# Causal attention on one NeuronCore: DRAM bounce laid out by component and head, first keys transposed into VectorE's PSUM bank

## What is computed

```python
q = einsum('bsm,hmd->bshd', resid, W_Q) + b_Q      # 32 heads of 32
k = einsum('bsm,hmd->bshd', resid, W_K) + b_K
v = einsum('bsm,hmd->bshd', resid, W_V) + b_V      # 256 values, 8 per head
q = _apply_rotary(q, sin, cos, 32)
k = _apply_rotary(k, sin, cos, 32)
k = concatenate([k, virtual_k], axis=1)            # 16 more keys
v = concatenate([v, virtual_v], axis=1)
scores = einsum('bqhd,bkhd->bhqk', q, k) / sqrt(32)
mask = arange(s + 16)[None, :] <= arange(s)[:, None] + 16
pattern = softmax(where(mask, scores, -inf), axis=-1)
z = einsum('bhqk,bkhr->bqhr', pattern, v_grouped)
out = einsum('bqhd,hdm->bqm', z, W_O)
```

## Time and profile before

| | us |
|---|---|
| median of 3 runs | 1694.87 |
| lowest and highest | 1694.71, 1704.96 |
| the profiled execution | 1699.04 |
| its span, from the first to the last instruction | 1697.2 |

### The profile page before, as it was taken

The page is one execution under the profiler, slowest core; times in us unless marked ns, Lnnn a source line. Parts: engine busy times, 40 slices in busy tenths (PEclk is TensorE's granted clock), DMA queues, the critical chain, the costliest instruction groups (busy, mean ns, idle before and its releaser), DMA issues. The chain is left out here.

```text
span 1697.2 us, 36694 instructions
## 1 busy us (share of the span) xinstructions
PE 1473.9 (87%) x12580; PEld 938.1 (55%) x12580; DVE 1234.0 (73%) x3703; ACT 1119.9 (66%) x2657; POOL 440.1 (26%) x442
## 2 busy tenths in 40 slices
PE   4688998989989885588888888769999999999996
PEld 2255555556555553366666666646555555555564
DVE  4367777777777765688888788663877878878755
ACT  1267676776767761567777677627888787887742
POOL 0333333333333313454544444330000000000001
PEclk9599999999999997899999999877999999999998
DMA  1677777788777745111001110007999999999920
GB/s 41 163 185 194 188 186 197 185 194 190 186 186 189 194 108 187 22 30 31 19 20 31 25 27 19 12 13 219 324 315 315 309 314 300 313 314 302 292 73 25
DMA packets 154904, 272.97 MB, mean 161 GB/s; under 512 B 27920, under 2 KB 31200, under 8 KB 154592
## 3 DMA queue, kind: packets, MB, share of 16 engines
q1 hardware_dynamic: 154720, 270.63, 56.3%
HBM read 148.03 MB, written 112.98 MB: 154 GB/s over the span
## 5 line engine op out<-in xcount | busy, mean ns | idle before, releaser
L519 ACT ACTIVATE a_Pm<-a_Pm,a_nm 128x272 f32<-128x272 f32 (+3 forms) x512 | 266.7, 570 | 167.3 <-DVE a_nm L441 166.7
L441 DVE CUSTOM_DVE_ANT_0 a_Pm<-ps,a_mask 128x272 f32<-128x272 f32 (+3 forms) x512 | 237.7, 503 | 92.3 <-PE ps L358 90.8
L1768 ACT COPY r_BD<-ps 128x320 f32<-128x320 f32 x512 | 200.4, 428 | 92.1 <-PE ps L1621 46.7
L1895 DVE CUSTOM_DVE_ANT_0 r_Sx<-ps,r_Sx 128x512 f32<-128x512 f32 x256 | 176.8, 691 | 108.8 <-PE ps L1634 107.2
L1621 PE MATMUL ps<-r_R,r_qv 32*128 32x320 f32 x1024 | 234.2, 498 | 3.2 <-ACT r_BD L1768 2.3
L358 PE MATMUL ps<-a_Kst,a_Qst 128*128 128x272 f32 (+4 forms) x640 | 200.6, 409 | 15.4 <-DMA a_Kst<-bounce 15.1
L1634 PE MATMUL ps<-r_K,r_qu 32*128 32x256 f32 x1024 | 199.7, 436 | 3.4 <-DVE r_nb L1895 3.4
L358 PEld LDWEIGHTS ps<-a_Kst,a_Qst 128*128 128x128 f32 x640 | 113.4, 193 | 146.3 <-issue 62.6
L1775 ACT ACTIVATE r_Sx<-r_Sx,r_nb 128x512 f32<-128x512 f32 x256 | 187.6, 733 | 7.9 <-DVE r_nb L1895 7.9
L1904 DVE COPY r_PT<-ps 128x512 f32<-128x512 f32 x256 | 175.9, 687 | 4.6 <-PE ps L1644 4.0
L373 PE MATMUL ps<-m_ident,a_Pm 128*128 128x128 f32 x1280 | 170.5, 278 | 1.6 <-ACT a_Pm L519 0.7
(11 more groups left out here) (204 smaller groups left out, 2745.9 us busy)
## 6 DMA issues: line engine op xcount, KB each, us to landing
spill<-r_BD SPq DMA_DIRECT2D x256, 288.0 KB, 5.0
r_Sx<-spill SPq DMA_DIRECT2D x128, 512.0 KB, 5.7
a_Kst<-bounce SPq DMA_DIRECT2D x128, 264.0 KB, 4.9
a_Qst<-bounce SPq DMA_DIRECT2D x128, 256.0 KB, 4.6
bounce<-a_kh SPq DMA_DIRECT2D x32, 264.0 KB, 3.5
bounce<-a_kl SPq DMA_DIRECT2D x32, 264.0 KB, 4.1
bounce<-a_qh SPq DMA_DIRECT2D x32, 256.0 KB, 5.7
bounce<-a_ql SPq DMA_DIRECT2D x32, 256.0 KB, 6.0
```

The lines of the kernel that those rows point to most:

```text
L441: nc.vector.tensor_tensor_reduce(out=Pm[:, u % 2, qt, 0:w], in0=S[:, S_of[qt]:S_of[qt] + w], in1=mask[:, N + AV - w:N + AV], scale=-SCALE, ...
L519: nc.scalar.activation(row, row, ACT.Exp, scale=-1.0, bias=nm[:, u % 2, qt:qt + 1]).then_inc(exp_done, 1)
L1768: nc.scalar.copy(BD[:, m % BUFS, j, HW * half:HW * half + HW], ps[:, BDB[k % 3], 0:HW]).then_inc(bd_ev, 1)
L1895: nc.vector.tensor_tensor_reduce(out=row, in0=ps[:, AC + n % 2, :], in1=row, scale=-SCALE, scalar=-BIG, op0=ALU.add, op1=ALU.min, accum_ou ...
```

## The change

Four things are rewritten, and no instruction is added or removed.

- `bounce` becomes (half, component, head, position) instead of (half, partition, position), and the tensors for queries have rows of 512 instead of 528.
- The stores to it now run over a destination view `h c n`: for each head, 32 components, one row each. The source is the same 128 partitions.
- `Qst` and `Kst` swap head and batch, so that the four heads of a batch lie side by side in a partition; a load reads one run of 4 x 512 or 4 x 528 numbers per component and writes one run per partition. The scores matmuls index accordingly.
- `first_transposes` writes to bank `TB + 1` and waits for VectorE's count `evd` instead of ScalarE's `eva`; the wait for `p0_ev`, which guards what follows in that bank, moves from part 0 of a unit's transposes to part 1.

```diff
-    Qst = [s.sb(f"Qst{i}", [P, GH, NB, N], F32R) for i in range(2)]
-    Kst = [s.sb(f"Kst{i}", [P, GH, NB, KN], F32R) for i in range(2)]
+    Qst = [s.sb(f"Qst{i}", [P, NB, GH, N], F32R) for i in range(2)]
+    Kst = [s.sb(f"Kst{i}", [P, NB, GH, KN], F32R) for i in range(2)]
...
-    bounce = [[nc.dram_tensor(f"bounce{k}{m}", (2, P, KN), F32, kind="Internal").ap() for m in range(4)] for k in range(2)]
+    bounce = [[nc.dram_tensor(f"bounce{k}{m}", (2, AD, GH, (N, KN)[m % 2]), F32, kind="Internal").ap() for m in range(4)] for k in range(2)]
...
             def stack(st, m):
                 i, k = m // 2, 4 * st + m
-                width_ = (N, KN)[m % 2]
                 dst, halves = ((Qst, (qh, ql)), (Kst, (kh, kl)))[m % 2]
                 for j, (src, made) in enumerate(zip(halves, (hi_done, lo_done))):
                     sp.wait_ge(made, k + 1)
-                    sp.dma_start(bounce[st % 2][m][j, :, 0:width_], src[:, i].bitcast(F32)).then_inc(bounced, 16)
+                    sp.dma_start(bounce[st % 2][m][j].rearrange("c h n -> h c n"), src[:, i].bitcast(F32)).then_inc(bounced, 16)
                 sp.wait_ge(bounced, 32 * (k + 1))
                 if st >= 2:
                     sp.wait_ge(s_ready, 2 * (U * (st - 2) + GH * (i + 1)))
                 for block, j in enumerate(((0, 1, 0, 1), (0, 0, 1, 1))[m % 2]):
-                    sp.dma_start(dst[st % 2][32 * block:32 * block + 32, :, i].bitcast(F32),
-                                 bounce[st % 2][m][j, :, 0:width_].rearrange("(h c) n -> c h n", h=GH)).then_inc(stk[st % 2][i], 16)
+                    sp.dma_start(dst[st % 2][32 * block:32 * block + 32, i].rearrange("c h n -> c (h n)").bitcast(F32),
+                                 bounce[st % 2][m][j].rearrange("c h n -> c (h n)")).then_inc(stk[st % 2][i], 16)
...
-                        ins = nc.tensor.matmul(S[:, lo:lo + w], q[:, h, i, P * qt:P * qt + P], k[:, h, i, at:at + w],
+                        ins = nc.tensor.matmul(S[:, lo:lo + w], q[:, i, h, P * qt:P * qt + P], k[:, i, h, at:at + w],
...
                     pe.wait_ge(exp_done, 4 * u + 4)
                     if u >= 1:
                         pe.wait_ge(evd, u)
+                    if u >= GH and u % GH == 1:
+                        pe.wait_ge(p0_ev, u // GH)
                 elif u >= 1:
                     pe.wait_ge(eva, 2 * u - (1 if k == 2 else 0))
-                if k == 0 and u >= GH and u % GH == 1:
-                    pe.wait_ge(p0_ev, u // GH)
...
                 pe.wait_ge(p0_done, GH * (bb + 1))
-                pe.wait_ge(eva, 2 * min(GH * (bb + 1) + 1, UNITS))
+                pe.wait_ge(evd, min(GH * (bb + 1) + 1, UNITS))
                 for qt in range(NT):
-                    ins = nc.tensor.transpose(ps[:, TB, P * qt:P * qt + P], P0[:, bb % 2, qt, :], c["ident"][:])
+                    ins = nc.tensor.transpose(ps[:, TB + 1, P * qt:P * qt + P], P0[:, bb % 2, qt, :], c["ident"][:])
...
-                nc.vector.tensor_copy(P0T[:], ps[:, TB, :]).then_inc(p0_ev, 1)
+                nc.vector.tensor_copy(P0T[:], ps[:, TB + 1, :]).then_inc(p0_ev, 1)
```

## The result

| | median us | runs | ratio to before, 95% interval |
|---|---|---|---|
| before | 1698.08 | 4 | |
| changed | 1948.69 (1945.62 to 1954.28) | 4 | 1.1474 [1.1423, 1.1524] |

The changed kernel is 251 us slower. (A fourth run of the kernel before moved its median from 1694.87 to 1698.08.) The forecast was slower with a chance of 0.92, at 2174 us, in a range of 1905 to 2255. So direction and range held, and the time forecast was 225 us too long; rival 1, with 1925 us, came closer than the forecast. The profiled execution of the changed kernel took 1954.28 us, its span is 1952.5.

A forecast was written before the change was run, and what follows sets the result against it. It took SP's serial chain of transfers in the attention stage as the bound. 483 - 3 - 1 = +479 us on the profiled 1699.04 gave 2178, less 4.2 for the median: 2174 us, range 1905 to 2255.

The forecast's parts named there:

- rival 1: Bounce stores: four engines don't collide, each at full 24.6 GB/s; pair 5.4 us, +3.65 per link, 1925 us; chance 0.25.
- What bounds the kernel: Attention stage: SP's serial chain of stack loads and bounce stores sets the pace, 63 links of 8.81 us; compute keeps up closely.
- The count of engines: Bounce stores: a destination of 4 outermost puts each store on four of the 16 DMA engines.
- The rate of four engines: Bounce stores: colliding engines take 9.3 us for a pair instead of 1.75; +7.55 us per link, +483 us over 64 pairs.
- The stack loads: Loads into Qst and Kst: longer runs gain zero; bounds no gain to -2.1 us per link.
- The first keys: P0 transposes: the wait for ScalarE goes, but a wait for the next landed stack covers it; -1 us.
- The start: Stage start: the first store begins ahead of the second, so some 3 us come off.
- Rival 4: PE: idle half of the time, its clock may stay at the lower level; 60 to 120 us more, 2234 to 2294; chance 0.07.

The follow-up runs named there:

- keys_only: The kernel before with only the first-key edits of the change (bank TB + 1, wait for VectorE); 1697.72 us, ratio 1.0013.
- early_hi: The kernel before with a semaphore for each half, so two of four loads are issued while the low half's store is under way; 1684.08 us, ratio 0.9934.
- early_hi_keys: The kernel before with a semaphore for each half, early loads of the high half, and the first-key edits; 1648.77 us, ratio 0.9721.
- halves: The kernel before with each bounce store of 128 partitions cut into two of 64; 1707.73 us, ratio 1.0075.
- runs_clean: The changed kernel with Qst and Kst laid out as before and a fifth, unused head in bounce, so loads move four runs on both sides; 1955.33 us, ratio 1.1527.
- four_blocks: The kernel before with a spare row after every 32 rows of bounce, so a store's destination is 4 x 32 rows; 1963.9 us, ratio 1.1604.
- short_runs: The changed kernel with Qst and Kst laid out as before, so a load writes four runs per partition; 1994.66 us, ratio 1.1782.

## Why the prediction was right or wrong

- *What bounds the kernel: right.* The chain of transfers on SP set the pace of the stage. Adding 3.92 us to a link cost 63 times that and 6.4 us at the start, 254 us in all. `keys_only` showed that compute's own gain is hidden. "A faster chain could gain little more than the waits within compute" was borne out by 11 us (`early_hi`) and 46 us (`early_hi_keys`).
- *The count of engines: right.* Four was taken from a copy of 127 rows that ran on one engine. Share 0.25, and 0.13 for a destination of 2, confirm it. The Trainium skill's rule ("DMA: Bandwidth & Descriptors", Why a DMA increments its semaphore by 16 and not by 1) gives 4 and 2 here, and the traces agree.
- *The rate of four engines: wrong, and it is the step that failed.* Two rows had shown sixteen engines at half their rate, and the prediction carried that over to four. It took "four fifths of the way" to 52 GB/s, a pair in 9.3 us, because it saw "nothing that would drive them apart". Measured are 94 to 104 GB/s and 5.4 us. The prediction had named 98 GB/s for 5.4 us as the sign of rival 1, and that is what came. The term was sized at +7.55 us a link and is +3.92: 3.63 x 64 = 232 us, a little more than the error of 225, of which the start, below, gives some back. The rows it rested on, 204 GB/s for the 64-partition copy and 209 for the stack, were transfers in which every engine handles few rows (64 and 32 over sixteen engines are 4 and 2 each, if dealt evenly). The halving itself is real: the halves run at 205 from idle. But carrying it to a walk over 32 rows per engine was a guess. Why four engines don't collide, no run shows; that they may fall out of step over a long walk is a reading. Rival 1 priced the other end, 3.65 us a link, and came within 0.27 us. That closeness is in part luck, for two misses offset each other: links that end in a Q set grew by 3.03 us, those that end in a K set by 4.79. A part of the K link's excess is seen in the one shown: its stores, which SP issues behind eight small ones, start when the loads have all but ended, and they start slowly, as the first pair did. In the last two rows they move 36 and then 82 GB/s.

```profile
319.00:320.00 1.00, 1.00 (x10) 0.95 (x9) 1.00 (x3) 1.00 (x4) 0.31 (x1) 1.00 0.51 99
320.00:321.00 1.00, 1.00 (x15) 0.60 (x13) 1.00 (x5) 0.34 (x2) 0.97 (x1) 1.00 0.15 36
321.00:322.00 1.00, 1.00 (x11) 0.54 (x4) 0.70 (x3) 0.97 (x2) 0.00 (x0) 1.00 0.24 82
```

- *The stack loads: right.* Zero was taken; the links of `runs_clean` and of the changed kernel are 12.73 and 12.74 us.
- *The first keys: right.* The wait went, and the wait for the stack took its place, as said.
- *The start: wrong, small.* 3 us were taken off for the first pair. That would have left 7.55 - 3 = 4.55 us for it. The first loads are issued at 63.44 and not at 57.08, 6.4 us later, more than one link's average of 3.92: the first store was issued 1.0 us later (54.71 against 53.72), and the pair moved at 36 GB/s for 2.5 us.
- *Rival 4, the clock: it fell, and cost nothing that can be seen.* The row of 250 to 400 us below has a granted clock of 0.83 and TensorE busy for 101.87 us. In the link above the clock is 0.53, near the lower level, right after a stretch of 4.50 us in which PE was not busy. Four units now have two links, 25.5 us, and half the clock in part of them stayed under the cover of the transfers.

```profile
250.00:400.00 150.00, 101.87 (x603) 67.20 (x603) 77.20 (x254) 71.87 (x155) 35.83 (x52) 0.83 0.52 132
```

## What to carry to other kernels

When a DRAM view is rearranged, look at the outermost number on both sides of each transfer, not only at run length and partitions: 128 partitions on one side don't help if the other side starts with 4, and the sign of it in a profile is a long wait beside a low DMA share. Before pricing a collision between engines, ask whether the rows that show it walk the data as the new transfer will; where they don't, give both ends a fair chance. And where two chains are nearly even, a gain in either one alone measures as little or nothing, so try them together before discarding one.

## What was not expected of the hardware

- One and the same pair of 64-partition stores ran at 205 GB/s from idle engines and at 361 GB/s behind other work, with the engines' share near 1 in both (`halves`).
- A store on four engines starts slowly from idle: 36 GB/s over the first 2.5 us in the changed kernel and 30 GB/s over an early stretch of 2 us in `four_blocks`, with a share of 0.24 in both. Later both run at some 100.
- The shape of a transfer changes what SP needs to issue it. Four loads took 2.50 us in `short_runs`, where one side can be described as 128 rows and the other as 32 x 4, and 1.70 to 1.75 in the changed kernel and in `runs_clean`. It goes with most of that run's loss: `short_runs` took 1994.66 us, and `runs_clean`, which differs by the spare head alone, 1955.33. A store of 128 partitions into 4 x 32 rows took 0.51 us, against 0.34 to 0.43 before; but two 64-partition stores of `halves`, with 64 rows on both sides, took 1.09, so unequal sides can't be the whole rule.
